# Six more waits of TensorE on its own products, in the hand-over from the shared layer to the routed experts

## The reference

```
x = x + xattn0(layernorm(x), ctx, ctx)          # softmax over features and over tokens
x = x + ffn0(layernorm(x))                      # low rank, silu(gate) * up
x = x + xattn1(layernorm(x), ctx)               # 16 heads, 4 key/value heads
x = x + moe(layernorm(x))

def moe(x):                                     # 16 experts, 4 for each token
    scores = sigmoid(x @ gate_w.T) + bias
    w, idx = top_k(scores, 4);  w = w / sum(w)
    z = silu(x @ Wg[e].T) * (x @ Wu[e].T)       # for each chosen expert e, width 256
    out = sum over e of  w[e] * z @ Wd[e].T
    return out + (silu(x @ Sg.T) * (x @ Su.T)) @ Sd.T     # the shared expert
```

## Time and profile before

| | |
|---|---|
| median of 3 runs | 682.33 us (682.24 to 683.34) |
| the profiled execution's own time | 682.37 us |
| its span, first to last instruction | 680.6 us |
| granted TensorE clock, mean | 0.995 |
| TensorE busy | 664.4 us, 98% of the span |

### The profile page before, as it was taken

How to read it: one execution, slowest core, us unless ns; L and a number is a source line. 1 busy time by engine, 2 the same in 40 slices (tenths; PEclk the granted TensorE clock), 3 DMA queues, 4 the chain that set the end, 5 groups by cost and what they waited for, 6 DMA issues and landing times.

```text
span 680.6 us, 9788 instructions
## 1 busy us (share of the span) xinstructions
PE 664.4 (98%) x2416; PEld 396.1 (58%) x2417; DVE 335.5 (49%) x867; ACT 220.1 (32%) x626; POOL 176.0 (26%) x226
## 2 busy tenths in 40 slices
PE   8999999999999999999999999999899999999993
PEld 6565444456777766777776777674444444444441
DVE  3995324433334556586766777455333333333331
ACT  5575522213344433545445463220111111111110
POOL 2366100001000000005414143356124332433334
PEclk9999999999999999999999999999999999999998
DMA  9999999331400200001104015313876757868554
GB/s 336 402 421 421 422 421 429 117 109 58 160 1 0 94 1 0 1 1 62 63 2 154 5 59 185 124 63 118 270 185 142 159 93 185 190 134 221 117 78 62
DMA packets 60403, 103.18 MB, mean 152 GB/s; under 512 B 7200, under 2 KB 32544, under 8 KB 59712
## 3 DMA queue, kind: packets, MB, share of 16 engines
q1 hardware_dynamic: 30320, 73.48, 29.0%
q0 software_dynamic: 8816, 18.00, 13.3%
q10 hardware_dynamic: 21232, 11.28, 5.8%
HBM read 46.60 MB, written 56.26 MB: 151 GB/s over the span
## 4 chain that ended last, share of the span: by engine, by line
PE 90%; DMA 3%; issue 3%; DVE 1%; ACT 1%; ACTq 1%; POOL 0%; POOLq 0%; SPq 0%; DVEq 0%
PE ps L1275 54%; PE ps L1470 12%; PE ps L1261 4%; PE ps L1439 4%; PE ps L1455 4%; PE ps L1386 3%; PE ps L1387 3%; PE ps L1396 3%; DMA out<-rq,sidx 1%; PE ps L1408 1%; DMA xr<-in_x 1%; PE ps L1322 1%; DMA rq<-slot_rows 1%; ACTq L444 0%; PE ps L1488 0%
## 5 line engine op out<-in xcount | busy, mean ns | idle before, releaser
L1275 PE MATMUL ps<-kv,rq 128*128 x432 | 192.4, 594 | 2.3 <-DVE rq L969 1.8
L1275 PE MATMUL ps<-zT,r 128*128 128x256 f32 (+1 forms) x552 | 132.5, 395 | 0.1
L1275 PEld LDWEIGHTS ps<-kv,rq 128*128 128x128 f32 x432 | 78.9, 190 | 89.2 <-issue 88.9
L1275 PEld LDWEIGHTS ps<-zT,r 128*128 128x128 f32 x552 | 103.5, 190 | 23.5 <-issue 10.1
L1470 PE MATMUL ps<-r 128*128 128x512 f32 x192 | 85.3, 593 | 0.0
L656 POOL DMA_INDIRECT out<-rq,sidx x36 | 56.7, 1574 | 108.6 <-DMA out<-rq,sidx 84.5
L581 POOL TENSOR_SCALAR ve<-mv 128x1 f32<-128x1 f32 x32 | 7.2, 224 | 261.6 <-DVE mv L988 261.6
L787 ACT ACTIVATE r<-ps,snm 128x128 f32<-128x128 f32 x128 | 45.3, 366 | 58.7 <-DVE snm L1104 57.5
L1200 DVE TENSOR_TENSOR rq<-ps,rq 128x256 f32<-128x256 f32 x36 | 15.3, 425 | 97.6 <-ACT rq L839 91.7
L1470 PEld LDWEIGHTS ps<-r 128*128 128x128 f32 x192 | 35.1, 190 | 37.8 <-issue 37.8
L839 ACT ACTIVATE rq<-ps 128x256 f32<-128x256 f32 x36 | 13.8, 384 | 119.2 <-PE ps L1275 109.3
(11 more groups left out here) (181 smaller groups left out, 862.9 us busy)
## 6 DMA issues: line engine op xcount, KB each, us to landing
slot_rows<-rq SPq DMA_DIRECT2D x4, 8192.0 KB, 50.6
kv<-in_experts SPq DMA_DIRECT2D x54, 256.0 KB
rq<-slot_rows ACTq DMA_DIRECT2D x138, 64.0 KB
r<-in_Wq SPq DMA_DIRECT2D x1, 3072.0 KB, 20.3
r<-in_Wo SPq DMA_DIRECT2D x2, 1536.0 KB, 6.4
r<-in_ctx SPq DMA_DIRECT2D x8, 256.0 KB, 8.4
xr<-in_x SPq DMA_DIRECT2D x8, 256.0 KB, 8.5
second_norm_rows<-zrow SPq DMA_DIRECT2D x8, 256.0 KB, 2.2
```

Of the source, the lines that this page charges most:

```text
L1275: mm = pe.matmul(out, lhs(k), rhs(k), start=(k == 0), stop=(k == n - 1))
```

## The change

Six waits are added on TensorE; nothing is moved, added or removed otherwise.

```diff
@@ sh_gu
                     if i == J - 2:
                         pe.wait_ge(s_p, NU)
+                    if i == J - 1:
+                        pe.wait_ge(s_hg, J - 1)
@@ sh_d
                     if j == 0:
                         pe.wait_ge(s_oc, NU)
                         pe.wait_ge(s_x3, J)
+                    if j == 2:
+                        pe.wait_ge(s_tr, len(TRN))
+                    if j == J - 3:
+                        pe.wait_ge(s_tabt, 1)
+                    if j == J - 2:
+                        pe.wait_ge(s_hd, j - 1)
@@ the first routed tiles
             gate_up(0, 0, *first)
             load, at = load_of(1), slot_of(1)
+            pe.wait_ge(s_hd, J)
             gate_up(1, 1, load, at)
```

## The result

| | before | after |
|---|---|---|
| median | 682.48 us (682.22 to 683.34, 6 runs) | 688.72 us (686.48 to 690.93, 6 runs) |
| the profiled execution's own time | 682.37 us | 688.33 us |

The ratio is 1.0095, with a 95% interval of 1.0079 to 1.011: slower, where the forecast said 0.3% faster. The time lies outside the forecast's range as well.

What follows compares the result with a forecast made beforehand. TensorE was taken to bound the kernel, with shifts before 486 us passing in full. Closing two hand-over holes gave 682.37 - 2.11 = 680.26 us, stated as 680.3; the range ran from 679.3 to 686.0.

Steps and rivals of the forecast that it cites:

- The bound and the passing of a shift: Routed tiles, 486 to 655 us: TensorE alone is busy throughout, so time lost or gained before comes out in full.
- TensorE's sequencer has less in hand while its products end: Hand-over, `tables` to `last_down`: added waits shorten TensorE's queue, so late signals become prompt; gain 2.11 us, chance 0.43.
- the contrast of two stretches: Signals prompt in routed rounds, where groups wait, but late in a bunch between `tables` and `last_down`, where three can be queued.
- The conditional's second half: With prompt signals, `turn(1)` and `turn(2)` come in time and the holes before `gate_up(1)` and `gate_up(2)` close: 2.11 us.
- the sum: Holes in front of `gate_up(1)` and `gate_up(2)` closed, 1.48 + 0.63 = 2.11 us, taken from 682.37 us.
- The covers: Work running ahead of each added wait, 1.6 to 3.4 us; with prompt signals (0.04 us) all six waits cost nothing.
- the bound of 2.5 us for the price of six waits: Upper price if every wait finds TensorE's array empty: 0.41 us each, six times; nothing was taken in the sum.
- the first rival: Lateness has another cause; `sh_d 6` stands waiting for `sh_d 4`: +3.6 us, 686.0. Chance of slower in all 0.33.
- The row on `tables`: ScalarE took up `tables` 3.2 us late though TensorE idled 0.44 us right behind it; named as speaking against the forecast.
- The rule of the Trainium skill: A matmul's semaphore is pushed when PSUM has acknowledged all bytes, so the waits bring no signal forward.
- decision point: Slower once the signal of `sh_d 4` comes after 470.8; until then the 1.48 us hole before `gate_up(1)` absorbs it.
- The wait for `tables`: `sh_d 5` would start at 468.6 against 467.59, costing 1.0 us more, counted inside the slower case's 3.6 us.

Runs made afterwards that it cites:

- e3: Kernel before, with GpSimd's last eight scatters of token numbers held back until the shared layer is done; 693.67 us, one run.
- e4: Kernel after, with GpSimd's last eight scatters of token numbers held back until the shared layer is done; 693.07 us, one run.
- e6: Kernel before plus only the wait of `sh_d 5` on `tables`; 682.36 us, ratio 1.0002 to before.
- e10: Kernel before, with only tile 5's token numbers scattered earlier, directly behind tile 5's row scatters; 686.18 us, ratio 1.0072 to before.
- e7: Kernel before, with three of the last eight token-number scatters moved between the rows of tiles 6 and 7; 685.72 us, ratio 1.0046 to before.
- e12: Kernel before, tile 5's token-number scatters moved behind the gate of tile 6, two of tile 6's behind its rows; 681.28 us, ratio 0.9986.
- e5: Kernel before plus only the wait of `sh_d 6` on `sh_d 4`; 687.37 us, ratio 1.0063 to before.
- e2: Kernel before plus four of the six waits, without those of `sh_d 5` on `tables` and `sh_d 6` on `sh_d 4`; 685.51 us, ratio 1.0052.
- e1: Kernel before plus only the waits of `sh_d 5` on `tables` and `sh_d 6` on `sh_d 4`; 688.74 us, ratio 1.0093.
- e8: Kernel after, with three of the last eight token-number scatters moved between the rows of tiles 6 and 7; 686.43 us, ratio 1.0056 to before.
- e11: Kernel after, with token numbers of tiles 5 and 6 scattered directly behind their own tiles' rows; 682.56 us, ratio 1.0015 to before.

## Why the prediction was wrong

**The bound and the passing of a shift** held: between 501 and 655 us TensorE is busy for 154.00 of 154.00 us in the kernel after too, and 5.1 of the 6.0 us arise before `gate_up(2)`.

**The step that failed** is "TensorE's sequencer has less in hand while its products end", with its conditional "if that is the cause". It rested on the contrast of two stretches that differ in the queue and in the scatters of token numbers alike, and I gave the queue the word. e3 and e4 show it is the scatters. The conditional's second half was sized about right: prompt signals are worth 2.5 us up to `gate_up(2)` (e3), where the sum had 2.11. The covers that I worked out for the six waits (1.6 to 3.4 us) were enough in e4, and too short where the signal is late by 7.1 us. So the bound of 2.5 us for the price of six waits was no bound: it priced an empty array, not the signal's lateness, although the row that showed the lateness (474.96) stood beside it.

**The argument against the first rival** was "the routed stage has scatters in every round and prompt signals". Those are other scatters, rows of the output, about one for each round of 5.4 us, with pauses; the late signals fall beside unbroken runs of eight to twelve scatters, 1.26 us apart. The row on `tables`, late with an almost empty queue, was the one that told the theories apart, and I gave it too little weight. The rule of the Trainium skill named there (Perfetto Trace Analysis, Tensor Engine Instruction) gave no gain from the waits, which was nearer, and the row on `tables` agreed with it.

**The first rival** had the mechanism, the place and the decision point: `sh_d 6` started at 474.67 (475.0 was said). It gave +3.6 us, 686.0, and the time was 688.33. Missing are two terms: the clock, which fell after 3.70 us without a product, +1.97 us, and a later round's wait, +0.84; the earlier start of `sh_d 6` is worth -0.33. That makes 3.6 + 1.97 + 0.84 - 0.33 = 6.08, against 5.96 measured; the 0.12 left are rounding and shifts of a few hundredths. With its chance at 0.33 and its price short, the range ended 2.3 us below the profiled execution.

**The wait for `tables`**, priced at +1.0 inside that sum, costs nothing that can be measured alone (e6). Here it makes a hole of 1.68 us; without it the wait on `sh_d 4` would have been longer by that, if the signal had come at the same moment, which no run shows.

## What to carry to other kernels

Before a wait is added, price it by the moment at which other engines take up that same signal in the trace, not by the end of the instruction that raises it; if the two are apart, find out what holds the signal first. Look for what else runs in every stretch where signals are late and is absent where they are prompt, and move that thing before the queue is blamed. And a hole of several microseconds on TensorE has a second price behind it, in the clock.

## What the runs showed of the hardware that I had not expected

- Signals of TensorE's products are taken up late while GpSimd issues long unbroken runs of small scatters. Most of the held ones are let go 0.7 to 2.2 us after the run's last scatter ends: 439.02 and 439.75 (e10), 458.03 and 459.84 (e7), 467.90 and 469.93 (e12), 473.20 and 474.96 (before), 472.52 and 474.61 (after). Others come through in the middle of a run: `gate 7` at 450.28, with no delay, and `tables` at 468.56, both before, and `sh_d 4` at 472.49 in e5, 1.4 us before the last scatter ends.
- The length of a run alone doesn't decide. Runs of four held nothing (e10), one of nine (e7, 461 to 472) and one of eight behind idle time (e3, from 473.66) let nearly all pass; runs of eight to twelve elsewhere held signals for up to 7.2 us. What fills up, and whether the signals are stopped or the sequencers that read them, stays open. SyncE, which waits for ScalarE's signal and not for TensorE's, is late as well, by 1.8 us (before) and 3.4 us (e7) against e3.
- The scatters' own work goes on behind their rows: in the kernel before, the load of the token numbers waits 3.12 us behind the last of them for their DMA. The Trainium skill (Perfetto Trace Analysis, DMA Instruction — SWDGE (GPSIMD)) says that the profiled end of such an instruction is that of making its descriptors, not of moving the data; the trace agrees. That most held signals are released only 0.7 to 2.2 us behind the row's end would fit it, but no run proves the link.
- The granted clock fell to half behind holes of 3.29 to 4.49 us (e5, e7, after, e2, e1), and stood at 1.00 behind that of 1.44 (e6). Shorter holes did either: 0.68 over the 5.30 us behind the hole of 2.21 in e12, 1.00 behind that of 2.13 in e10; and around `tables`, behind holes of 1.43 and 0.44 us, 0.58 for 3.80 us in e8 and 1.00 in e11. So the length of the last hole alone doesn't decide. Behind the holes of 3.29 to 4.49 us the price was 1.6 us (e2) to 3.0 us (e7).
